# Top-16 attention: queries and keys of eight heads in 128 rows instead of twice 128, with biases loaded as columns

## What is computed

```python
pos = conv over tokens, per feature, 3 taps (pos_w), zero padding
x = x + pos + pos_b
q, k, v = split(x @ qkv_w.T + qkv_b)          # 8 heads of 16 features each
logits = einsum('bmd,bpd->bmp', q * 128 ** -0.5, k)
_, idx = top_k(logits, 16)                    # per head and query, of the sequence's 1024 keys
attn = softmax over the 16 chosen keys
out = (attn @ v of the chosen keys), heads side by side
h = h + out @ wo_w.T + wo_b
```

## Time and profile before

| | us |
|---|---|
| median of 3 runs | 1485.04 (1481.46 to 1486.34) |
| profiled execution | 1487.46 |
| its span | 1485.7 |
| this stage, first GpSimd instruction of its block to its last | 629.2 to 1256.6 |

### The profile page before, as it was taken

One profiled execution on the slowest core, in us unless ns is written; L12 is line 12 of the kernel. 1 busy time (PEld: TensorE's weight loads), 2 busy tenths in 40 slices (PEclk: granted clock), 3 DMA queues, 4 the chain that ended last, 5 costly groups with the idle time before them and its releaser, 6 DMA issues. The chain is left out here.

```text
span 1485.7 us, 29930 instructions
## 1 busy us (share of the span) xinstructions
PE 1156.4 (78%) x10544; PEld 803.5 (54%) x10544; DVE 1154.7 (78%) x2164; ACT 655.5 (44%) x1184; POOL 657.5 (44%) x569
## 2 busy tenths in 40 slices
PE   5878999998589987888777777777777775758661
PEld 3735666665479976645444444444444444547551
DVE  4676766562625589589999999999999995767884
ACT  4253434332125422156555555555555552014661
POOL 2033325230276762235555555555555554207144
PEclk9889999999689989899999999999999997969995
DMA  4090000000248610000000000000000000004782
GB/s 135 1 266 2 2 2 3 2 2 2 63 136 230 200 36 1 1 1 1 1 0 0 0 0 0 0 0 0 0 0 0 0 1 0 3 5 131 217 232 75
DMA packets 83644, 65.02 MB, mean 44 GB/s; under 512 B 14203, under 2 KB 74005, under 8 KB 83285
## 3 DMA queue, kind: packets, MB, share of 16 engines
q1 hardware_dynamic: 63124, 46.86, 11.5%
q10 hardware_dynamic: 16320, 8.40, 1.9%
q0 software_dynamic: 4096, 8.40, 1.8%
HBM read 43.70 MB, written 22.28 MB: 44 GB/s over the span
## 5 line engine op out<-in xcount | busy, mean ns | idle before, releaser
L1202 POOL TENSOR_TENSOR ta_ex<-ta_ex,ta_left 128x1024 f32<-128x1024 f32 x128 | 301.6, 2356 | 261.3 <-DVE ta_left L1251 261.3
L1021 PE MATMUL ta_ps_s<-ta_kT,ta_qz 128*128 (+1 forms) x512 | 255.2, 623 | 0.3 <-ACT ta_ex L1129 0.3
L1071 PE MATMUL ta_ps_t<-consts,ta_ex 128*128 128x128 f32 x1024 | 144.4, 286 | 140.6 <-POOL ta_ex L1202 138.2
L1071 PEld LDWEIGHTS ta_ps_t<-consts,ta_ex 128*128 128x128 f32 x1024 | 113.7, 144 | 229.5 <-POOL ta_ex L1202 206.2
L1235 DVE MAX8 ta_top<-ta_ps_s 128x8 f32<-128x1024 f32 x128 | 154.7, 1209 | 4.2 <-PE ta_ps_s L1021 4.2
L1241 DVE MATCH_REPLACE8 ta_left<-ta_etop,ta_ex 128x1024 f32<-128x1024 f32 x128 | 153.5, 1200 | 0.0
L1246 DVE MAX8 ta_second<-ta_left 128x8 f32<-128x1024 f32 x128 | 153.5, 1199 | 0.0
L1251 DVE MATCH_REPLACE8 ta_left<-ta_second,ta_left 128x1024 f32<-128x1024 f32 x128 | 153.5, 1199 | 0.0
L1129 ACT ACTIVATE ta_ex<-ta_ps_s,ta_ntop 128x1024 f32<-128x1024 f32 x128 | 140.3, 1096 | 0.0
L1021 PEld LDWEIGHTS ta_ps_s<-ta_kT,ta_qz 128*128 128x128 f32 x512 | 89.7, 193 | 74.6 <-issue 71.2
L2962 ACT ACTIVATE l1h_score<-l1h_work 128x2048 f32<-128x2048 f32 (+1 forms) x40 | 68.5, 1712 | 106.4 <-PE l1h_work L2769 106.4
(11 more groups left out here) (639 smaller groups left out, 2546.4 us busy)
## 6 DMA issues: line engine op xcount, KB each, us to landing
l1f_arena<-in_L_ffn_W_dram SPq DMA_DIRECT2D x46, 256.0 KB, 3.7
l3e_packed<-l3f_packed SPq DMA_DIRECT2D x64, 160.0 KB, 2.9
l3f_rows<-l1f_zero SPq DMA_DIRECT2D x2, 2048.0 KB, 13.3
l3e_x<-l3f_rows SPq DMA_DIRECT2D x32, 128.0 KB
l3e_outs<-l3e_y ACTq DMA_DIRECT2D x32, 128.0 KB, 3.1
l1f_rows<-l1f_zero SPq DMA_DIRECT2D x2, 1472.0 KB, 9.4
l1f_arena<-l1f_rows SPq DMA_DIRECT2D x46, 64.0 KB, 3.6
l1e_outs<-l1e_y ACTq DMA_DIRECT2D x46, 64.0 KB, 3.0
```

Of the source, the lines that this page charges most:

```text
L1021: ins = pe.matmul(ps_s[:, i % 2, half * BANK:(half + 1) * BANK], qz[:, odd, h, :], kT[:, grp, bass.ds(at.key0[i // PAIR] + half * BANK, BA ...
L1071: ins = pe.transpose(ps_t[:, j * P:(j + 1) * P], ex[:, i % 4, j * P:(j + 1) * P], m.ident)
L1202: pool.tensor_tensor(ex[:, i % 4, :], ex[:, i % 4, :], left[:, i % 4, :], ALU.subtract).then_inc(kept, 1)
```

## The change

Queries and keys stay as the weights give them: head h has rows 16h to 16h+15, and all eight heads fill 128 rows. `qT` and `kT` become `[128, 2048]`, a sequence has 4 projections instead of 8, and they multiply with the plain weights `wqkv3`. The mask has eight columns (`m.eighth`), one for each head's 16 rows. The biases of query, key and value come by one load as three columns of a `[128, 3]` tile, which ScalarE and the matmul on L1088 read. `wpad`, `bpad`, `brow`, `qkvb` and what fills them go. Both first query products of GpSimd now wait for the first projection only. The late projections lie in items 0 to 3 (`LATE = 4`); the late value projections stay in items 0 to 7.

```diff
-        r.wpad = sb("wpad", [P, 2, 2, P])
-        r.bpad = sb("bpad", [P, 2, 2])
+        r.wo_b, r.b = sb("wo_b", [1, D]), sb("b", [P, 3])
...
         def fetch(sp):
...
-            sp.dma_start(r.qkvb[:, :], row(w["L2_ffn_qkv_b"])[:, 0:2 * D]).then_inc(loaded, 16)
-            sp.dma_start(r.bv[:, :], col(w["L2_ffn_qkv_b"])[2 * D:3 * D, :], allow_slow_non_contiguous=True).then_inc(loaded, 16)
+            sp.dma_start(r.b[:, :], w["L2_ffn_qkv_b"].rearrange("(k p) -> p k", p=P), allow_slow_non_contiguous=True).then_inc(loaded, 16)
...
         def pad(pool):
             pool.memset(r.v[:, :, :, TW:TW + 1], 1.0)
-            pool.memset(r.wpad[:, :, :, :], 0.0).then_inc(padded, 1)
-            pool.memset(r.brow[:, :, :, :], 0.0).then_inc(padded, 1)
-            pool.wait_ge(loaded, 80)
-            pool.wait_ge(padded, 2)
-            for kind in range(2):
-                pool.tensor_copy(r.wpad[...], m.wqkv3[...])
-                pool.tensor_copy(r.brow[...], r.qkvb[...])
+            pool.wait_ge(loaded, 64)
             pool.tensor_scalar(r.posw[:, 1:2], r.posw[:, 1:2], 1.0, None, ALU.add)
...
-            kind, grp, half = [(0, 0, 0), (1, 0, 0), (1, 0, 1), (0, 1, 0), (1, 1, 0), (1, 1, 1), (0, 0, 1), (0, 1, 1)][k]
+            kind, half = [(0, 0), (1, 0), (1, 1), (0, 1)][k]
...
-                return pe.matmul(bank, r.wpad[:, kind, grp, :], r.xc[:, tokens], start=True, stop=True)
+                return pe.matmul(bank, m.wqkv3[:, kind, :], r.xc[:, tokens], start=True, stop=True)
...
-                if i < FIRST:
+                if i < LATE:
                     if i >= 1:
                         pe.wait_ge(late_done, i)
                     project(1, i, ps_p[:, :]).then_inc(late_ready, 1)
...
-            for n in range(4):
-                pe.matmul(ps_p[:, n:n + 1], r.brow[0:1, n // 2, n % 2, :], m.one[0:1, 0:1], start=True, stop=True)
-            pe.matmul(ps_p[0:1, P:2 * P], r.bv[:, :], m.wo[:, :], start=True, stop=True).then_inc(b_ready, 1)
+            pe.matmul(ps_p[0:1, P:2 * P], r.b[:, 2:3], m.wo[:, :], start=True, stop=True).then_inc(b_ready, 1)
             spin(pe, m, ps_s[:, 0, 0:BANK], 4)
             pe.wait_ge(conv_step, 3)
             for k in range(3):
                 project_first(k)
-            pe.wait_ge(b_in, 2)
+            pe.wait_ge(b_in, 1)
             project_first(3)
             pe.wait_ge(proj_done, 3)
             for i in range(2):
                 logits(place(pe, 0), i, True)
-            for k in range(4, 8):
-                pe.wait_ge(proj_done, k - 3)
-                project_first(k)
-            pe.wait_ge(proj_done, 6)
...
-            act.wait_ge(b_in, 1)
-            for k in range(5):
-                keep_projection(k)
-            keep_projection(5)
+            for k in range(4):
+                keep_projection(k)
             exponentials(place(act, 0), 0)
-            keep_projection(6)
             exponentials(place(act, 0), 1)
-            keep_projection(7)
...
-            for grp in range(2):
-                pool.wait_ge(proj_done, (1, 4)[grp])
-                pool.tensor_tensor(qz[:, 0, 4 * grp:4 * grp + 4, :], qT[:, grp, 0:P]..., m.quarter...)
+            pool.wait_ge(proj_done, 1)
+            for some, signal in ((slice(0, 4), q_first), (slice(4, 8), q_in)):
+                pool.tensor_tensor(qz[:, 0, some, :], qT[:, 0:P]..., m.eighth[:, some]...).then_inc(signal, 1)
-            pool.wait_ge(proj_done, 8)
+            pool.wait_ge(proj_done, 4)
...
-                    dve.tensor_copy(r.bpad[:, :, :].rearrange("p a b -> p (a b)"), ps_p[:, 0:4]).then_inc(b_in, 1)
```

More of the change, by code:

```diff
@@ L67 @@
 RET_H, RET_D = 8, 64
-CONST_COLS = {"ident": 128, "interp": 128, "pairmean": 128, "one": 128, "pid": 1, "plain": 1, "quarter": 4, "order": 16,
+CONST_COLS = {"ident": 128, "interp": 128, "pairmean": 128, "one": 128, "pid": 1, "plain": 1, "eighth": 8, "order": 16,
               "expand": 256, "before": 128, "firsts": 32, "ropecos": S, "ropesin": S}
@@ L100, in constants @@
     out["plain"] = np.where(np.isin(np.arange(P), (0, 107, 108, 109)), 0.0, np.sqrt(float(D))).astype(np.float32)[:, None]
-    out["quarter"] = (np.arange(P)[:, None] // 32 == np.arange(4)[None, :]).astype(np.float32)
+    out["eighth"] = (np.arange(P)[:, None] // 16 == np.arange(8)[None, :]).astype(np.float32)
     out["order"] = np.broadcast_to(np.arange(16, 0, -1, dtype=np.float32), (P, 16))
@@ L885, in stage_l2_ffn @@
         r.v = sb("v", [P, TILES, TH, TW + 1])
-        r.wpad = sb("wpad", [P, 2, 2, P])
-        r.bpad = sb("bpad", [P, 2, 2])
[L888 to L891, removed]
+        r.wo_b, r.b = sb("wo_b", [1, D]), sb("b", [P, 3])
+        r.posw, r.posb = sb("posw", [P, 3]), sb("posb", [P, 1])
+        loaded = signals(nc, m, "t_")("loaded")
         def fetch(sp):
@@ L928, in topk_attend @@
     SC = float(D) ** -0.5
-    PAIR, FIRST, AHEAD = 2 * TH, 8, 4
+    PAIR, FIRST, LATE, AHEAD = 2 * TH, 8, 4, 4
     KEPT = 4
@@ L936, in topk_attend @@
         sem = signals(nc, m, "ta_")
-        qT, kT = sb("qT", [P, 2, N]), sb("kT", [P, 2, N])
+        qT, kT = sb("qT", [P, N]), sb("kT", [P, N])
         vseq = sb("vseq", [P, CH, TH, 2 * TW])
@@ L997, in projected @@
         def projected(seq, k):
-            kind, grp, half = [(0, 0, 0), (1, 0, 0), (1, 0, 1), (0, 1, 0), (1, 1, 0), (1, 1, 1), (0, 0, 1), (0, 1, 1)][k]
-            tokens = slice(seq * S + half * BANK, seq * S + (half + 1) * BANK)
-            return kind, grp, tokens
+            kind, half = [(0, 0), (1, 0), (1, 1), (0, 1)][k]
+            return kind, slice(seq * S + half * BANK, seq * S + (half + 1) * BANK)
         start_banks = [ps_t[:, 0:BANK], ps_t[:, BANK:2 * BANK], ps_o[:, :], ps_p[:, :]]
@@ L1008, in project @@
             def project(seq, k, bank):
-                kind, grp, tokens = projected(seq, k)
-                return pe.matmul(bank, r.wpad[:, kind, grp, :], r.xc[:, tokens], start=True, stop=True)
+                kind, tokens = projected(seq, k)
+                return pe.matmul(bank, m.wqkv3[:, kind, :], r.xc[:, tokens], start=True, stop=True)
             def logits(at, i, begin=False):
                 h, odd, n = i % TH, (i // TH) % 2, at.item0 + i
-                grp = h // 4
                 if begin:
@@ L1021, in logits @@
                     ins = pe.matmul(ps_s[:, i % 2, half * BANK:(half + 1) * BANK], qz[:, odd, h, :],
-                                    kT[:, grp, bass.ds(at.key0[i // PAIR] + half * BANK, BANK)], start=True, stop=True)
+                                    kT[:, bass.ds(at.key0[i // PAIR] + half * BANK, BANK)], start=True, stop=True)
                 ins.then_inc(s_ready, 1)
@@ L1080, in step @@
                 if i == FIRST - 1:
-                    pe.wait_ge(late_done, FIRST)
+                    pe.wait_ge(late_done, LATE)
             def project_first(k):
-                project(0, k, start_banks[k % 4]).then_inc(proj_ready, 1)
-            for n in range(4):
-                pe.matmul(ps_p[:, n:n + 1], r.brow[0:1, n // 2, n % 2, :], m.one[0:1, 0:1], start=True, stop=True)
-            pe.matmul(ps_p[0:1, P:2 * P], r.bv[:, :], m.wo[:, :], start=True, stop=True).then_inc(b_ready, 1)
+                project(0, k, start_banks[k]).then_inc(proj_ready, 1)
+            pe.matmul(ps_p[0:1, P:2 * P], r.b[:, 2:3], m.wo[:, :], start=True, stop=True).then_inc(b_ready, 1)
             spin(pe, m, ps_s[:, 0, 0:BANK], 4)
@@ L1108, in _ @@
             pe.wait_ge(v_done, 1)
-            pe.wait_ge(proj_done, 8)
+            pe.wait_ge(proj_done, 4)
             pe.wait_ge(conv_step, 6)
@@ L1119, in copy_projection @@
             def copy_projection(seq, k, bank):
-                kind, grp, tokens = projected(seq, k)
-                return act.activation((qT, kT)[kind][:, grp, tokens], bank, ACT.Identity, bias=r.bpad[:, kind, grp:grp + 1])
+                kind, tokens = projected(seq, k)
+                return act.activation((qT, kT)[kind][:, tokens], bank, ACT.Identity, bias=r.b[:, kind:kind + 1])
             def exponentials(at, i):
@@ L1171, in keep_projection @@
                 act.wait_ge(proj_ready, k + 1)
[L1172 to L1175 removed]
+                copy_projection(0, k, start_banks[k]).then_inc(proj_done, 1)
+            for k in range(4):
                 keep_projection(k)
[L1177 removed]
             exponentials(place(act, 0), 0)
[L1179 removed]
             exponentials(place(act, 0), 1)
[L1181 removed]
             act.wait_ge(v_ready, 1)
@@ L1191, in query @@
             def query(at, tile_rel):
-                for grp in range(2):
-                    ins = pool.tensor_tensor(qz[:, tile_rel % 2, 4 * grp:4 * grp + 4, :],
-                                             qT[:, grp, bass.ds(at.pair * (2 * P) + tile_rel * P, P)].unsqueeze(1).broadcast_to([P, 4, P]),
-                                             m.quarter.unsqueeze(2).broadcast_to([P, 4, P]), ALU.mult)
+                for some in (slice(0, 4), slice(4, 8)):
```

(17 more changed lines are left out.)

## The result

The changed kernel took 1477.05 us (median of 22 runs, 1475.56 to 1482.29), the kernel before 1481.48 (22 runs, 1475.96 to 1486.34): ratio 0.9977, 95% interval 0.9966 to 0.9988, a gain of 3.4 us (1.8 to 5.0); the two medians lie 4.4 us apart.

What follows compares the result with a forecast made beforehand. VectorE, without a gap in top-16 attention, was taken to bound the kernel, so its run's start counts. The sum 3.6 + 0.4 - 1.0 = 3.0 us from 1485.04 gave 1482.0 us, range 1478.4 to 1485.6.

Steps and rivals of the forecast that it cites:

- The level: Starting time of the whole kernel before the change: median of three runs, 1485.04 us, from which the gain was subtracted.
- Up to the first logits nothing moves: Start of top-16 attention: first maximum stays at 640.13 and second at 641.94, gain nothing.
- First term: Start of top-16 attention: four projections leave TensorE's queue, VectorE's unbroken run starts 3.6 us sooner (0 to 4.7).
- Late half: Items 0 to 7: four projections and copies of sequence 1 go, hidden beside busy VectorE, gain nothing.
- Second term: Layernorm before the stage: GpSimd's padding work no longer slows VectorE's normalising pass, gain 0.4 us (0 to 0.6).
- The clock: TensorE before the projections: longer idle stretch may bring the low clock level, 1.0 us lost (0 to 1.7, or 2.7).
- The shared port: Last convolution pass: GpSimd's two query products may keep VectorE out, 0.4 us to spare, cost nothing.
- The sum: Whole kernel: 3.6 + 0.4 - 1.0 = 3.0 us gained, median 1482.0 us; 2 to 4 us gained has chance 53%.
- clock kept: Rival: projections stay at the high clock level or executions before suffer as much, 4.2 us gained, 1480.8; chance 25%.
- hidden anyway: Rival: value path holds item 2, or low clock takes 2.7 us or more; gain about 0.6 us, 1484.4; chance 16%.
- slower: Rival: low clock holds from 634.2 to the logits of item 2; 4.4 us slower, 1489.4; chance 5%.
- does not do what it says: Rival: the halved projections stay on the queue; chance 1%.

Runs made afterwards that it cites:

- before_again: The kernel before, unchanged, measured again against itself: ratio 1.0006 (0.9987 to 1.0025).
- first pair: One profiled execution each of the kernel before and the changed kernel, as first measured: ratio 0.9977.
- pad_work: Changed kernel with GpSimd's old clears of padded weights and a row, and four copies, put back in the layernorm: ratio to the kernel before 0.9993.
- spin_on: Changed kernel with two more spins of two matmuls, behind the first and second convolution pass: ratio to the kernel before 0.9968.
- bias_back: Changed kernel with four one-row matmuls, results not used, put back ahead of the spin: ratio to the kernel before 0.9998.
- second pair: The kernel before and the changed kernel, both without an edit, profiled once more: changed to before ratio 0.9990 (0.9975 to 1.0004).

## Why the prediction was right or wrong

- *The level: wrong.* "For the median I get 1482.0 us" took the median of three runs, 1485.04, as the level, with the words that it moves "by more than 1 us by itself". It lay 3.6 us above the median of 22 and 5.4 above that of all 122. This is the step that put the result outside the range: of the 4.95 us, 3.56 are the level, and 1.4 that the two medians lie 4.4 us apart and not 3.0. The range went down only 3.6 us from the forecast, for "the whole gain with a fast median", and so had no room for a level that is off by that much. The trace had a sign of it: the granted clock was 0.95 in the earlier trace rows, and I read that as the engine's normal state. The forecast difference, put on 1481.48, gives 1478.5; the range then should have been some 3 us wider below.
- *Up to the first logits nothing moves: wrong by the clock alone.* M1 grew from 10.90 to 12.21.
- *First term, 3.6 us: right.* The distance from the first to the third maximum fell by 3.78, of which 0.35 is the lower clock of the first execution: against before_again it fell by 3.43, and putting the projections back cost 3.45 and 3.48. The remaining idle time was forecast as 1.1 and is 0.99.
- *Late half, nothing: right*, to 0.02 us.
- *Second term, 0.4 us: a size.* The pass went to 4.19 as said; L fell by 0.26 in the first pair and 0.13 in the second, and `pad_work` puts 0.20 to 0.47 on the same work. One execution each is little for this: with the changed layernorm L is 11.57 to 11.84 in eight traces, at a granted clock near 0.85, and 10.47 in the one at 1.00.
- *The clock, 1.0 us lost: mis-sized.* The idle stretch came out at 2.70 (forecast 1.5 to 2.8), the loss at 1.3 and 1.6 by M1 of the two pairs and 1.5 by the experiments. The 1.7 weighed beside it by the rule of the Trainium skill, "TensorE: Matmul & The Clock Gate", section "What's actually happening", is nearer; the trace agrees that with less activity before them the projections ran at the low level.
- *The shared port, nothing: right*, and by another order. In the changed kernel the convolution pass was first and GpSimd's two products took 2.51 us instead of about 2.1; VectorE lost nothing. Where the order was as forecast, in `spin_on` and `bias_back`, the pass took 1.95 us and the two products 3.12: by these lengths VectorE was kept out for the first product and got in before the second. What I passed over is the first clear: the row showed 2.31 against 0.80 us, and I used it only as evidence on the products, though it stood on the path.
- *The sum.* 3.45 + 0.3 - 1.5 = 2.25 us from the experiments' sizes, against 3.0 forecast, 2.99 between the first two profiles, and 3.4 (1.8 to 5.0) in the time. The second pair gave 1.28 us between the profiles and 1.5 in the time (0.9990), so that 3.0 was met so closely is in part luck. Of the rivals, "clock kept" is out by the traces, "hidden anyway" (0.6 us) by the first comparison and by the distances, "slower" and "does not do what it says" by both.

## What to carry to other kernels

Where one engine runs without a gap, ask only when that run begins; then follow the queue that releases its last idle stretch, since a wait shown on another engine can be cover for it. Before taking away work without use on TensorE, look at how long the engine will then stand idle before work that is on the path. And before setting a range on a 0.2% change, look whether the granted clock of long unchanged stretches differs between executions, and give the level its own width.

## What was not expected of the hardware

In the same code, ahead of the changed stage, the high level of TensorE's clock was granted at 0.95 over 185 us in one execution and at 0.99 to 1.00 in the other eleven traces; that one reached the stage 2.3 to 7.8 us after them. A clear of 1.80 us on GpSimd held a VectorE pass of 0.80 us for 1.5 us. Ahead of the projections TensorE was at its low level after an idle stretch of 2.70 us in all six profiles that had one, and at its high level after 1.75 us in the one that had that. Idle time is not all of it: in the kernel before, the level fell during the spin, in both profiles, with nothing longer than 0.93 us idle in that block.
